# Result rows of a fused attention and feed-forward kernel: written by ScalarE instead of GpSimd

## The reference, cut to what matters

```python
x = layernorm(h + attn(h))                    # eps 1e-5, no weight or bias
x = layernorm(x + (x @ ternary_weight.T * scale + bias))
```

## Time and profile before

| what | value |
|---|---|
| median of 3 runs | 418.98 us (415.02 to 420.5) |
| the profiled execution, its own time | 418.8 us |
| its span in the trace | 417.0 us |
| busy: PE, DVE, ACT, POOL | 366.6, 327.7, 285.9, 302.5 us |
| busy shares of the span | 88%, 79%, 69%, 73% |
| mean granted TensorE clock | 0.971 of full speed |

### The profile page before, as it was taken

One profiled execution on the slowest core, in us unless ns is written; L12 is line 12 of the kernel. 1 busy time (PEld: TensorE's weight loads), 2 busy tenths in 40 slices (PEclk: granted clock), 3 DMA queues, 4 the chain that ended last, 5 costly groups with the idle time before them and its releaser, 6 DMA issues. The chain is left out here.

```text
span 417.0 us, 8782 instructions
## 1 busy us (share of the span) xinstructions
PE 366.6 (88%) x3109; PEld 296.8 (71%) x3111; DVE 327.7 (79%) x663; ACT 285.9 (69%) x818; POOL 302.5 (73%) x190
## 2 busy tenths in 40 slices
PE   6995797958989889999999999989899999989771
PEld 5994585646859677776868787868677787868650
DVE  3686779677889998898979797999999898943411
ACT  4657764685876969696968595876969696956200
POOL 1845352074797989888979787998989898968615
PEclk9999889988999999999999999999999999999896
DMA  7993002687676775767576758787776757584350
GB/s 251 319 262 110 1 0 24 180 307 139 102 124 117 112 126 92 141 88 140 92 129 85 127 102 124 106 128 136 106 142 100 137 90 134 97 130 63 56 72 26
DMA packets 150285, 50.22 MB, mean 120 GB/s; under 512 B 138592, under 2 KB 148832, under 8 KB 149984
## 3 DMA queue, kind: packets, MB, share of 16 engines
q1 hardware_dynamic: 149424, 49.32, 63.1%
q10 hardware_dynamic: 816, 0.33, 0.3%
HBM read 11.87 MB, written 4.19 MB: 39 GB/s over the span
## 5 line engine op out<-in xcount | busy, mean ns | idle before, releaser
L1207 POOL TENSOR_TENSOR ao<-room_wg,ao 128x1024 f16<-128x1024 f32 x32 | 68.3, 2134 | 17.0 <-ACT ao L706 16.9
L666 PE MATMUL PS<-V,room_wg 128*128 128x129 f32 x512 | 69.0, 286 | 10.8 <-POOL room_wg L1217 4.5
L1217 POOL TENSOR_TENSOR room_wg<-room_comp,keep 128x1024 f32<-128x1024 f32 x32 | 74.7, 2356 | 1.9 <-ACT room_comp L822 1.9
L666 PEld LDWEIGHTS PS<-V,room_wg 128*128 128x128 f32 x512 | 62.7, 197 | 16.0 <-POOL room_wg L1217 7.0
L831 ACT ACTIVATE room_h<-PS,room_K 128x8 f32<-128x8 f32 (+7 forms) x256 | 70.8, 376 | 1.4 <-DVE room_K L1056 1.1
L831 ACT ACTIVATION_READ_ACCUMULATOR room_h<-PS,room_K 128x1 f32 x256 | 63.5, 262 | 0.0
L1223 POOL TENSOR_TENSOR ny<-nx,nu 128x16 f32<-128x16 f32 x16 | 46.7, 2916 | 22.2 <-DVE nx L1032 22.2
L632 PE MATMUL PS<-Weff,aoT 128*128 128x256 f16 x512 | 60.8, 273 | 0.4 <-DMA aoT<-ao 0.4
L632 PEld LDWEIGHTS PS<-Weff,aoT 128*128 128x128 f16 x512 | 49.8, 98 | 8.4 <-DMA aoT<-ao 1.1
L589 PE MATMUL PS<-room_h,kT 128*128 128x512 f16 x192 | 47.6, 380 | 9.2 <-DMA room_h<-room_K 8.3
L1030 DVE TENSOR_REDUCE ssq<-room_wg 128x8 f32<-128x1024 f32 x30 | 36.5, 1219 | 17.3 <-ACT room_wg L775 16.9
(11 more groups left out here) (181 smaller groups left out, 740.2 us busy)
## 6 DMA issues: line engine op xcount, KB each, us to landing
H<-in_L_attn_h SPq DMA_DIRECT2D x4, 512.0 KB, 6.3
room_wg<-in_L_attn_Wg SPq DMA_DIRECT2D x1, 2048.0 KB, 14.3
cw_rows<-staged SPq DMA_DIRECT2D x1, 2048.0 KB, 6.4
CW<-cw_rows SPq DMA_DIRECT2D x1, 2048.0 KB, 7.8
aoT<-ao SPq DMA_TRANSPOSE x128, 2.7
out<-room_wo SPq DMA_DIRECT2D x16, 128.0 KB, 2.0
CW<-in_L_attn_Wq_up SPq DMA_DIRECT2D x2, 512.0 KB, 13.1
room_wo<-in_L_attn_Wo SPq DMA_DIRECT2D x1, 1024.0 KB, 14.6
```

Source lines behind the costliest of these rows:

```text
L666: last = nc.tensor.matmul(pv, Pm[:, c, 2 * pr:2 * pr + 2, :], V[:, 2 * i + c, :], start=True, stop=True)
L1207: G.tensor_tensor(ao16[:, 1, c, :, :], ao[:, c, :, :], ao16[:, 0, c, :, :], ALU.subtract).then_inc(g_al, 1)
L1217: G.tensor_tensor(Pm[:, c, :, :], E[:, c, :, :], keep[:, :, :], ALU.mult).then_inc(g_mask, 1)
```

## The change

The result rows (z - m) * r are written by ACT as Identity(z * r + shift), one ACTIVATE with a scale and a bias per row. POOL writes the shift, -m * r, one 128x1 instruction behind the small power, in every step that has an ffn part. POOL no longer writes result rows. On ACT, `results(i-3)` stands between `query_high` and `output_high(0)` in the middle steps. In step 16, `results(13)` stands first, ahead of `feed_forward_high`, and `results(14)` last; in step 17 `results(15)` is last. The semaphore g_out is replaced by a_out, and the new one g_sh orders the shift.

```diff
@@ sync
-                    sp.wait_ge(g_out, tile + 1)
+                    sp.wait_ge(a_out, tile + 1)
@@ scalar, step
+                def results(tile):
+                    act.wait_ge(g_sh, tile + 1)
+                    act.wait_ge(s_out, 16 * tile + 16)
+                    nc.scalar.activation(res[:, :], zs[tile % 2], ACT.Identity, bias=shift[:, 0:1],
+                                         scale=ny[:, HEADS + 1:HEADS + 2]).then_inc(a_out, 1)
+                if i == NT:
+                    results(NT - 3)
                 if front and i < 1:
                     square(i + 1, 0)
...
+                    for tile in stored(i):
+                        results(tile)
                     output_high(0)
...
                     output_high(1)
+                if i >= NT:
+                    results(i - 2)
@@ vector, step
-                    wait(dve, g_out, i - 3)
+                    wait(dve, a_out, i - 3)
...
-                        wait(dve, g_out, i - 2)
+                        wait(dve, a_out, i - 2)
@@ gpsimd, step
-                def results(tile):
-                    pool.wait_ge(g_rl, tile + 2)
-                    pool.wait_ge(s_out, 16 * tile + 16)
-                    G.tensor_scalar(res[:, :], zs[tile % 2], mv[:, 1, 0:1], ny[:, HEADS + 1:HEADS + 2], ALU.subtract,
-                                    ALU.mult).then_inc(g_out, 1)
-                if i == NT:
-                    results(NT - 3)
...
-                    for tile in stored(i):
-                        results(tile)
...
                     pool.wait_ge(g_rl, i)
+                if ffn:
+                    G.tensor_scalar(shift[:, :], mv[:, 1, 0:1], ny[:, HEADS + 1:HEADS + 2], -1.0, ALU.mult,
+                                    ALU.mult).then_inc(g_sh, 1)
                 if proj:
...
-                for tile in stored(i) if not mid else ():
-                    if tile != NT - 3:
-                        results(tile)
```

More of the change, by code:

```diff
@@ L115, in build @@
         v_unit, w_unit, v_inv, w_inv = (unit[:, n:n + 1] for n in range(4))
-        ckn, ckw = sb("ckn", [P, 1]), sb("ckw", [P, 1])
+        ckn, ckw, shift = (sb(n, [P, 1]) for n in ("ckn", "ckw", "shift"))
         fsum, fscale, fthr, fthn = (sb(n, [P, 1]) for n in ("fsum", "fscale", "fthr", "fthn"))
@@ L196, in build @@
             "p_q", "p_sw", "p_cs", "p_o", "p_pv", "p_ct", "p_xt", "p_f"))
-        a_sq, a_tanh, a_es, a_ec, a_qt, a_ct, a_at, a_xt = (sem(n) for n in (
-            "a_sq", "a_tanh", "a_es", "a_ec", "a_qt", "a_ct", "a_at", "a_xt"))
+        a_sq, a_tanh, a_es, a_ec, a_qt, a_ct, a_at, a_xt, a_out = (sem(n) for n in (
+            "a_sq", "a_tanh", "a_es", "a_ec", "a_qt", "a_ct", "a_at", "a_xt", "a_out"))
         d_nq, d_nl, g_rs = sem("d_nq"), sem("d_nl"), sem("g_rs")
@@ L205, in build @@
             "d_red", "d_qn", "d_rope", "d_add", "d_cmax", "d_rc", "d_ql", "d_ao", "d_fr", "d_y", "d_xl"))
-        g_mask, g_cn, g_al, g_rl, g_x1, g_xb, g_out = (sem(n) for n in (
-            "g_mask", "g_cn", "g_al", "g_rl", "g_x1", "g_xb", "g_out"))
+        g_mask, g_cn, g_al, g_rl, g_x1, g_xb, g_sh = (sem(n) for n in (
+            "g_mask", "g_cn", "g_al", "g_rl", "g_x1", "g_xb", "g_sh"))
         s_out, s_qt, s_ah, s_al = sem("s_out"), sem("s_qt"), sem("s_ah"), sem("s_al")
```

## The result

The changed kernel takes 427.49 us in the median of four runs (427.04 to 428.78), the kernel before 417.58 us, also in the median of four; the ratio is 1.024, 95% interval 1.016 to 1.032. Measured once more with more runs, it was 1.0247 (1.0201 to 1.0292). It is slower in both, and only the second interval lies wholly above 2%. A ratio is reckoned without the executions that fell in a slower state, and can differ by a few tenths of a per cent from the quotient of two medians. The forecast was 429.7 us, slower. The profiled execution took 427.04 us with a span of 425.2 us, against 418.8 and 417.0 before.

What follows compares the result with a forecast made beforehand. No engine is full; a loop of waits from step to step sets the end. Middle steps 0, step 16 +10.98, last steps -0.06 give +10.9 us on 418.8, so 429.7 us; range 426 to 433.

Steps and rivals of the forecast that it cites:

- Step 16, the placement: Head of ACT's step 16: the wait for tile 12's store delays feed_forward_high and tile 15's projection, 10.98 us.
- the clock's share: Step 16, PE after its 12 us pause: lower clock level again; nothing added, up to +1.5 us for a longer stretch.
- L639's wait of 0.90: PE in step 16: L639's earlier wait for a transpose disappears, so 0.90 us of the 11.88 us delay is got back.
- The middle steps, the gain: Steps 3 to 15: without POOL's result rows, L1147's three held cases go, gaining 1.2 us (range 0 to 16).
- The middle steps, the shift's cost: POOL's 0.25 us shift makes the large power 0.16 us late in seven middle steps: 1.1 us, between 0 and 3.3.
- the sum of 0: Middle steps together: -1.2 + 1.1, taken as 0, between -2 and +4 us.
- ACT's new instruction: 128x256 ACTIVATE with two per-row operands: 0.57 us, filling ACT's 0.66 us gap ahead of output_high(0), cost 0.
- The last chain: Steps 16 and 17: shift before x1 of tile 15 +0.25, last result row on ACT -0.31, together -0.06 us.
- The covered wait (1): Step 16: tile 12's store lands before ACT gets there, so only small terms remain, 418.7 us; 5%.
- POOL as the bound (2): POOL bounds the middle steps: 13 x 0.98 = 12.7 us gained against step 16's loss, 417.0 us; 5%.
- Rival 3: Middle steps lose: the shift costs 0.56 us and the 1.2 us gain doesn't come, 433.3 us; 10%.
- middle steps that differ by more than 0.3 us: Sign against the forecast: such steps would mean the loop runs through POOL's result rows or ACT's gap.

Runs made afterwards that it cites:

- experiment 1: Changed kernel with ACT's result rows of tile 13 moved behind the high part of tile 14 in step 16: 416.97 us, ratio 0.9946 to the kernel before.
- experiment 2: Kernel before plus only a wait on ACT for the store of tile 12 at step 16, POOL still writing all result rows: 427.09 us, ratio 1.0155.
- experiment 3: Changed kernel, order kept, but ACT writes result rows into input tile H's place, so no wait for the store: 417.87 us, ratio 0.9973.
- experiment 9: Four kernels side by side: changed 1.0247; before with the wait for tile 12's store 1.0208, for tile 11's 1.0000; changed with high part first 0.9949.
- experiment 8: Kernel before, with POOL writing only one of 256 result columns in the middle steps: 417.46 us, ratio 0.9974.
- experiment 5: Changed kernel with high part first, plus POOL's shift moved behind the masks, in step 16 to POOL's head and behind x1 plus bias: 416.76 us, ratio 0.9971.
- Experiment 4: Changed kernel with high part first, plus three more 128x1 POOL instructions beside the shift in steps 2 to 15: 421.29 us, ratio 1.0059.
- Experiment 7: Changed kernel with high part first, plus ACT writing each middle result row twice: 416.93 us, ratio 0.9977.

## Why the prediction was right, point by point

- **Step 16, the placement.** Right in mechanism and in nearly all of its size: 10.98 us forecast, 9.93 measured in the profile. Experiments 1, 2, 3 and 9 show it from four sides: move the high part out from behind the wait, add the wait alone, take it away, lower its threshold. Two terms of it were off, in opposite directions. The store landed 2.04 us after its issue (398.59 to 400.63), where the step took over 3.41 from the kernel before, 1.37 less. And L623 took 5.30 us for 4.76, 0.54 more; the text had named the clock's share as 0 to 1.5 and added nothing. PE did come back at the lower level, as forecast, but L623's length also changes from profile to profile with no such pause (see above). The reckoning said that the projection would be late by ACT's delay less L639's wait of 0.90; measured, the high part is 11.44 us behind `output_high(1)` where it was 0.96 (391.85 - 390.89), so 10.48 for ACT's delay, and from it to L1148 it is 12.35 us instead of 12.90, 0.55 less (0.90 back, 0.54 lost on L623, 0.19 in the gaps): 9.93. The profiles of the other runs bear it out. From L1148 (L1135) of step 15 to that of step 16 it takes 26.23 to 27.35 us in the four profiles in which ACT waits for the store of tile 12 ahead of the high part, and 16.53 to 17.72 in the ten others.
- **The middle steps, the gain.** L1147's three long cases are gone in the changed kernel (L1160 there, 0.17 us each). What the forecast made of it, 1.2 us, is inside the noise: experiment 8 shows -1.1 with an interval from -2.8 to +0.6. Not shown as a size.
- **The middle steps, the shift's cost.** The step that failed: "There the power comes some 0.25 - 0.11 + 0.02 = 0.16 us late, 7 x 0.16 = 1.1 us". The shift's length was right (0.26 us), the holding was there (0.12 us, in five of the seven steps), and the power came 0.10 us late, but the step behind it was not longer by it (18.33 us for 18.34), and moving the shift away gains nothing (experiment 5). What was wrong was the path: a power that is late by so little is not in the loop. What leaves the room of about 0.2 us on POOL's way is open; a wait of PE for a query transpose may be it, but no run shows that. Experiment 4 shows that beyond the room the cost is real, 4.3 us for 14 x 0.74. Gain and cost had been set against each other, so the sum of 0 came near though one of its terms was not paid and the other cannot be told from noise: that part was luck.
- **ACT's new instruction.** 0.57 us forecast, 0.59 to 0.60 measured. The Trainium skill's figures (ScalarE: Activation LUTs, What ACT_TABLE_LOAD costs) made it an estimated 0.585, and the trace agrees. In step 12 ACT's idle time ahead of `output_high(0)` shrank from 0.66 us (as in step 11) to 0.18; in steps 4 and 10 none was left. Experiment 7 shows that even a second copy has room.
- **The last chain.** -0.06 forecast; POOL's shift put x1 0.25 us later and the last result row's end is 9.55 us after L1148's start, where it was 9.45. Against the forecast another 0.25 us went into L560, 0.69 us for 0.44, with the granted clock at 0.63 in that window (416 to 418 us) and 0.90 before (408 to 410). The last store then landed 0.63 us faster.
- **The rivals.** The covered wait (1) is out by the 9.88 us that ACT stood. POOL as the bound (2) is out by experiment 8. Rival 3, losing middle steps, is out as it was put: experiment 1 is below the kernel before, and the shift can be moved without gain.

**What stays open.** The prediction named middle steps that differ by more than 0.3 us as a sign against it, and one does: in the changed kernel the step from 312.76 to 332.77 is 20.01 us long, 19.32 before. That ACT's result rows are the cause is not shown. In the kernels with them the step was 19.34 to 20.01 us, in those with POOL's 19.04 to 19.86, and the 19.86 belong to the kernel before with only the wait for the store of tile 11, in which nothing of the middle steps is changed. Less than 2 us before this step's L1032 (L1045) PE has waited for a query transpose, for 1.73 us in the changed kernel and 1.51 in that one; in the kernel before it was 0.62 us; why the transpose lands late was not tried. Over all middle steps it is the same. From the L1032 of step 1 to L1135 of step 15 (by their lines in the kernel before) four profiles with the middle steps of before give 282.96 to 284.75 us, and five with the changed ones 283.68 to 285.14. A cost of the change there of some tenths of a microsecond can't be told from this scatter.

## What to carry to other kernels

When work moves to another engine, its waits move with it: look first at what is queued behind the waiting instruction there, in the steps where the overlap has ended. The rest of this change could not be told from neutral; one wait whose 9 us had been free on GpSimd was paid almost in full on ScalarE, for 1 of the 16 tiles. Putting the needed instruction ahead of the wait, one line moved, turned a loss of 2.5% into a gain of 0.5%.

## What the runs showed of the hardware that was not expected

The store of tile 12, the same 128 KB behind the same transposes, took 3.41 us from issue to landing in the kernel before, where PE went on running L632 for 2.1 us after the issue, and 2.04 us in the changed kernel, where PE stood idle. The twelve profiles in which the landing can be read fall in these two groups. In five, PE ran L632 for about 2 us after the issue, and the store took 3.11 to 3.65 us. In seven, L632 was not running at the issue or ended within 0.2 us of it (among them experiments 4, 7 and 8), and it took 1.98 to 2.17 us. In the kernel before, the DMA share in the window from 400 to 402 us was 1.00 at only 46 GB/s:

```profile
400.00:402.00 2.00, 1.88 (x18) 1.44 (x15) 0.00 (x0) 0.00 (x0) 0.00 (x0) 1.00 1.00 46
```

In the changed kernel the store was issued at 398.59 and landed at 400.63, and the two windows are these:

```profile
398.00:400.00 2.00, 0.00 (x0) 0.00 (x0) 0.00 (x0) 0.00 (x0) 0.00 (x0) 0.50 0.61 114
400.00:402.00 2.00, 0.00 (x0) 0.00 (x0) 0.40 (x1) 0.87 (x2) 0.00 (x0) 0.50 0.07 24
```

This is a pattern and not a cause: what fills the DMA engines there was not tried.

A DVE instruction of 0.17 us can be held by a running GpSimd instruction and shows as a longer instruction, not as idle time: 1.00 us in experiment 4, ending when POOL's `output_low(1)` does. In the profiles of before, after and experiments 1 and 4 there are 21 such long cases of the two DVE instructions that release POOL's powers, and each ends 0.02 to 0.04 us after POOL's `output_low`. It would be missed in the list of waits.
